# Two graph layers on one core: the message pass as one pipeline, the verdict beside the last strip, and normalising on ScalarE

## The chip, the cores and the metric

One core of a Trainium2 chip runs the whole program. The metric is the device time of one execution in microseconds (us). Differences of about 0.2% (5 us) are the least that a measurement of this kernel can tell from no change.

## The reference

6250 nodes with 128 features, 200,000 edges sorted by target node `dst` (skewed: low nodes have many edges), 32 attributes for each edge.

```python
edge_index = stack([src, dst])
h = maximum(layernorm(x), 0)
x = x + L0(h, edge_index)            # gcn_conv, relu, gcn_conv
h = maximum(layernorm(x), 0)
x = x + L1(h, edge_index, edge_attr)
# gcn_conv: segment_sum((x @ W)[src] * dinv[src] * dinv[dst], dst) + b, self loops included
# L1:  msg = relu(concat(x[src], edge_attr) @ W1 + b1)
#      agg = segment_sum(msg, dst) / max(count, 1)
#      relu(concat(x, agg) @ W2 + b2)
```

## The kernel before, in words

The program is one chain of stages, written out engine by engine. SP, ACT and POOL issue DMAs; order on each engine is the order of the code, and engines meet only at semaphores.

1. **Setup** (to about 240 us): node starts are searched in the sorted target list, features of the first layernorm are made, and a slot is worked out for each of the first 98,304 edges (24 ranges of 32 tiles of 128 edges).
2. **Counts and first convolution** (240 to 960 us): `shared(0)` builds, strip by strip (25 strips of up to 256 targets), a matrix of edge counts (L1083 on PE, one-hots on DVE at L2067 and L2071, eviction on ACT at L1416), and applies it to the node table (L1095). The last strip is short (112 targets) and is applied alone, 49 blocks of 3 matmuls.
3. **Verdict** (`verdict`, L2151 to L2170): DVE checks that the counts are exact, that every range fits, and so on; two small matmuls on PE (L1161, L1162) gather what the partitions found; the result is `flag`. Every engine waits for `flag_ready` 4 and reads the flag: 0 (the case here) takes the fast path, 1 a general one (`full`).
4. **Second convolution**: `node_phase(1)` and `shared(1)`, which loads the stored counts, widens them (L578, L580) and multiplies (L1110), to 1290 us.
5. **Third node phase** (`node_phase(2)`, 1290 to 1362 us, 13 groups of 4 node blocks): for each group PE turns the sums back (`back`), DVE adds x (L1906), takes mean and variance (L1714, L1719), ACT takes the root (L1336), DVE inverts it (L1880) and normalises with four instructions (L1885); PE turns (L947), ACT applies relu twice (L1346, L1349), PE multiplies (L983), DVE adds the bias and makes the rows of the message table (L1919), SP stores them, ACT clears (L1372).
6. **Messages** (`messages_mixed`, 1360 to 2447 us). Two kinds of work run interleaved.
   - *Ranges.* The 98,304 edges whose rows POOL has **scattered** into blocks (L814: 24 ranges x 32 indirect DMAs, issued between stages 2 and 5 with `pace` waits that keep them from running ahead). A range is 49 tiles, handled in 14 **units** of 4 or 3 tiles, 24 x 14 = 336 units. Per unit: ACT stages the attributes (L1511), PE turns them (L1211), ACT takes them (L1518), PE makes products and picks source rows by a one-hot (L1218, L1222; the one-hot on DVE at L2249), ACT and DVE split the message (L1525, L2239), DVE builds the target one-hot (L2254), PE sums (L1234). Per range: the blocks are loaded by SP (`load_blocks`, L634), prepared on DVE (L1892), their low parts turned on PE, stored and loaded again spread over the partitions by ACT (`store_lows`, `load_lows`, L1500), and the sums folded, turned and added.
   - *Chunks.* The other 102,400 edges, 200 chunks of 4 tiles. POOL **gathers** each tile's source rows with one indirect DMA (`gather_messages`, L796: 800 of them), at most 8 chunks ahead of their use and held further by `rows_added` and `pre_ready`. Per chunk: half of an 8-matmul group on PE (L1187), DVE adds (L2262), ACT relu (L1505), one-hot (L2211), PE sums (L1196), DVE adds into the result (L2219).
   - *Order.* `pair_of` writes the order of two ranges (28 units) as 30 **steps**, with 16 chunks spread over them. A hardware loop (`Fori`) runs it 11 times, and a twelfth copy has the last pair with 24 chunks. Steps 28 and 29 of each pair only finish what steps 26 and 27 began, and the next pair's first unit starts behind them. The spread low parts of the next pair's first range are loaded at steps 27, 28 and 29; those of the second range at steps 10, 12 and 14. POOL's 800 gathers are written out, without a loop.
7. **Last phase** (2450 to 2495 us): the update matmuls (L1289, L1292) and the output.

Of the kernel before, what the change touches and what calls it, by code (L numbers as in the profile page):

```python
# [6 lines left out]
F32 = mybir.dt.float32  # L7
# [8 lines left out]
P = 128  # L16
# [74 lines left out]
LO_TURNED_AT = (7, DU + 10)  # L91
LO_LOADED_AT = ({DU - 4: (0, 1), DU - 2: (2,), DU: (3,)}, {2 * DU - 1: (0, 1), 2 * DU: (2,), 2 * DU + 1: (3,)})
FIRST_TURN = DT // (SLOTS * TC)
PAIRS = RANGES // 2
PAIR_UNITS = 2 * DU
PAIR_TURNS = 2
PAIR_CHUNKS = PAIR_TURNS * SLOTS
LAST_CHUNKS = (TURNS - FIRST_TURN) * SLOTS - (PAIRS - 1) * PAIR_CHUNKS
MESSAGE_CHUNKS = (PAIRS - 1) * PAIR_CHUNKS + LAST_CHUNKS
PAIR_STEPS = PAIR_UNITS + 2  # L100
PREPARED_AT = (5, DU + 8)
# [32 lines left out]
EXACT = 256.0  # L134
EPS = 1e-5
# [3 lines left out]
assert DT % (SLOTS * TC) == 0 and LAST_CHUNKS % SLOTS == 0 and RANGES % 2 == 0 and DU % 2 == 0 and sum(UNIT_TILES) == SB and RT % 2 == 0  # L139
# [7 lines left out]
def build(nc, t, out):  # L147
    with ExitStack() as ctx:
# [203 lines left out]
        rstd = sb("rstd", [P, 2, GB])  # L352
        eps = sb("eps", [P, 1])
# [170 lines left out]
        def chunk_of(u, chunks):  # L524

            c = u * chunks // PAIR_STEPS
            return c if (u + 1) * chunks // PAIR_STEPS > c else None
# [55 lines left out]
        def _(sp):  # L583
# [49 lines left out]
            def load_blocks(k, j):  # L633
                sp.dma_start(landed[j], permuted[bass.ds(k * (2 * RANGE_ROWS) + j * RANGE_ROWS, RANGE_ROWS), :].rearrange("(p b) c -> p b c", p=P)  # L634
                             ).then_inc(B[f"landed_{j}"], 16)
# [5 lines left out]
            def load_mixed():  # L641

                def load_pair(k, turns, last):
                    for i in range(turns):
                        for h in range(2):
                            sp.wait_ge(rows_added, k * PAIR_CHUNKS + (i * SLOTS + HALF * h + HALF + 2))
                            load_attributes(k * PAIR_TURNS + (i + 1), h)
                            if (i, h) == (1, 0) and not last:
                                sp.wait_ge(B["prepared"], k * 2 + 1)
                                sp.sem_inc(held["sp"], 1)  # L650
                                sp.wait_ge(B["staged"], k * PAIR_UNITS + DU)
                                load_blocks(k + 1, 0)
                    if not last:
                        sp.wait_ge(B["prepared"], k * 2 + 2)
                        sp.sem_inc(held["sp"], 1)
                        sp.wait_ge(B["staged"], k * PAIR_UNITS + PAIR_UNITS)
                        load_blocks(k + 1, 1)

                for j in range(2):
                    sp.wait_ge(scattered[j], RANGES // 2 * RT * 16)  # L660
                with sp.Fori(0, PAIRS - 1) as k:
                    load_pair(k, PAIR_TURNS, False)
                load_pair(PAIRS - 1, LAST_CHUNKS // SLOTS - 1, True)
# [76 lines left out]
            load_blocks(0, 0)  # L740
            sp.dma_start(message_rows, t["src_t"][:, DT:NT]).then_inc(message_inputs_loaded, 16)
            load_blocks(0, 1)
# [152 lines left out]
        def _(pe):  # L895
# [218 lines left out]
            def shared(n):  # L1114
# [4 lines left out]
                if n == 0:  # L1119
# [20 lines left out]
                    for h in range(SB):  # L1140
                        apply((STRIPS - 1) % 2, h, LAST_WIDTH)
# [18 lines left out]
            pe.wait_ge(flag_ready, 1)  # L1160
            mm(ps_turn[0:1, 0:P], found[:, 0:1], ident, start=True, stop=True).then_inc(flag_ready, 1)  # L1161
            mm(ps_extra[0:1, 0:1], found[:, 3:4], ones[:, 0:1], start=True, stop=True).then_inc(flag_ready, 1)  # L1162
            pe.wait_ge(flag_ready, 4)
            flagged = pe.value_load(flag[0:1, 0:1], min_val=0, max_val=1)
            with pe.If(flagged > 0):
                full(0)
            node_phase(1)
# [4 lines left out]
            def messages_mixed():  # L1172
# [6 lines left out]
                def products_of(k, c):  # L1179

                    pe.wait_ge(rows_added, k * PAIR_CHUNKS + c + 2)
                    if c % HALF == 0:
                        pe.wait_ge(attr_loaded[c % SLOTS // HALF], (k * PAIR_TURNS + c // SLOTS) * 16 + 16)
# [7 lines left out]
                def sums_of(k, c):  # L1191
                    pe.wait_ge(msgs_ready, k * PAIR_CHUNKS + c + 1)
                    pe.wait_ge(e["added"], k * PAIR_CHUNKS + c + SLOTS)
                    pe.wait_ge(e["onehot"], k * PAIR_CHUNKS + c + 1)
# [5 lines left out]
                def turn_lows(k, r):  # L1200

                    pe.wait_ge(B["prepared"], k * 2 + r + 1)
                    pe.wait_ge(B["added"], k * 2 + r + 1)
                    pe.wait_ge(B["lo_evicted"], k * 2 + r + 1)
                    mm(ps_turn[0:SB, 0:P], block_lo[r][:, 0:SB], ident_bf[:], start=True, stop=True).then_inc(B["lo_turned"], 1)

                def turn_attr(k, u):

                    n = unit_tiles(u % DU)[1]
                    pe.wait_ge(B["staged"], k * PAIR_UNITS + u + 1)  # L1210
# [3 lines left out]
                def block_products(k, u):  # L1214

                    b0, n = unit_tiles(u % DU)
                    pe.wait_ge(B["attr"], k * PAIR_UNITS + u + 1)
                    mm(banks[u % 3][:, 0:n * D], attr_turned[u % 2][0:n * DE, :], edge_w[0:n * DE, 0:n].rearrange("p j d -> p (j d)"),  # L1218
                       start=True, stop=False, skip_group_check=True)
                    pe.wait_ge(B["source"], k * PAIR_UNITS + u + 2)  # L1220
# [5 lines left out]
                def block_sums(k, u):  # L1226

                    n = unit_tiles(u % DU)[1]
                    pe.wait_ge(B["rest"], k * PAIR_UNITS + u + 1)
                    pe.wait_ge(B["target"], k * PAIR_UNITS + u + 1)  # L1230
                    if u % DU == 0:
                        pe.wait_ge(B["folded"], k * 2 + u // DU + 1)
# [5 lines left out]
                def turn_sums(k, before, before_lows=True):  # L1238

                    pe.wait_ge(B["folded"], k * 2 + before + 1)  # L1240
                    pe.wait_ge(B["added"], k * 2 + before + 1)
                    if before_lows:
                        pe.wait_ge(B["lo_evicted"], k * 2 + before + 2)
                    nc.tensor.transpose(ps_turn[:, 0:P], range_sums, ident).then_inc(B["sums_turned"], 1)

                def pair_of(k, chunks, last):
                    for u in range(PAIR_STEPS):
                        c = chunk_of(u, chunks)
                        if c is not None and c % 2 == 0 and (not last or c + 2 < chunks):
                            products_of(k, c + 2)  # L1250
                        if u < PAIR_UNITS:
                            turn_attr(k, u)
                        if c is not None:
                            sums_of(k, c)
                        if 1 <= u <= PAIR_UNITS:
                            block_products(k, u - 1)
                        if u == TURNED_SUMS_AT:
                            turn_sums(k, 0)
                        if u == DU + TURNED_SUMS_AT:
                            turn_sums(k, 1)  # L1260
                        if 2 <= u:
                            block_sums(k, u - 2)
# [1122 lines left out]
```

## Time and profile before

| | |
|---|---|
| three runs | 2489.32, 2491.26, 2493.92 us; median 2491.26 |
| profiled execution | 2496.99 us, its span 2494.8 us |
| PE busy | 2175.6 us (87%), 15568 matmuls |
| DVE busy | 1886.4 us (76%) |
| POOL busy | 1824.0 us (73%), 1687 instructions |
| ACT busy | 1219.0 us (49%) |

"Busy" counts execution only. An engine's time between two instructions is listed apart, with what ended it (the releaser). "Issue" as a releaser means that the engine waited for nothing that the profile shows: its own instruction stream had to come forward. So an engine that is busy 73% of the time need not have been free for the other 27%.

### The profile page before, as it was taken

Reading aid. Unit: us, or ns where it says so; the run is one execution under the profiler, and the core shown is the slowest. Engines: PE = TensorE matmul, PEld = TensorE weight load, DVE = VectorE, ACT = ScalarE, POOL = GpSimd, SP = SyncE. Lnnn points to the kernel's source line nnn. Section 1 sums busy time; section 2 is a strip of 40 time slices with the busy share of each in tenths; the row PEclk is TensorE's granted clock in tenths of the full one; section 3 lists DMA queues with packets and bytes.
Section 4 is the critical chain, followed back from the end, with each engine's and each line's share of the span. In section 5 each row is a group of like instructions: output and inputs, shape, how many; then the busy total and the mean of one; then the engine's idle time right before and its main releaser. Section 6 shows DMA issues by size and latency. Waiting matters only on the chain.

```text
span 2494.8 us, 47576 instructions
## 1 busy us (share of the span) xinstructions
PE 2175.6 (87%) x15568; PEld 1787.8 (72%) x15569; DVE 1886.4 (76%) x3609; ACT 1219.0 (49%) x3297; POOL 1824.0 (73%) x1687
## 2 busy tenths in 40 slices
PE   0355799999999996899985899999999999999996
PEld 0133689997668995788874677877877877787785
DVE  6999999998889884544447677776777777777776
ACT  5845246665667773555543343433433443444440
POOL 0858777888888877777777777777777776777770
PEclk9666999999999998999997899999999999999998
DMA  9414133343333432688873334334343433434332
GB/s 365 162 41 160 48 125 125 133 156 118 135 136 125 183 128 61 231 306 323 308 263 87 105 117 136 108 117 124 101 127 115 127 109 102 136 101 128 115 91 61
DMA packets 127167, 357.85 MB, mean 143 GB/s; under 512 B 34082, under 2 KB 77831, under 8 KB 117687
## 3 DMA queue, kind: packets, MB, share of 16 engines
q10 hardware_dynamic: 24752, 186.56, 19.8%
q0 software_dynamic: 56880, 85.25, 13.1%
q1 hardware_dynamic: 45369, 84.00, 9.8%
q8 instruction: 83, 1.36, 0.2%
q14 instruction: 83, 0.68, 0.1%
HBM read 229.75 MB, written 125.93 MB: 143 GB/s over the span
## 4 chain that ended last, share of the span: by engine, by line
PE 67%; DVE 15%; DMA 5%; issue 4%; POOL 4%; ACT 4%; DVEq 1%; ACTq 0%; POOLq 0%; SPq 0%
PE ps_feat L1095 6%; PE ps_sum L1196 6%; PE ps_node L1095 6%; PE ps_node L1110 5%; PE ps_feat L1110 5%; DVE region_c L2071 5%; PE ps_extra L1234 5%; PE ps_node L1218 4%; PE ps_node L1222 4%; DMA rows_or_lows<-block_lows 3%; ACT rows L1310 3%; PE ps_sum L1222 3%; PE ps_feat L1218 3%; PE ps_sum L1218 3%; PE ps_feat L1222 3%
## 5 line engine op out<-in xcount | busy, mean ns | idle before, releaser
L814 POOL DMA_INDIRECT permuted<-rows_or_lows,slot_of_edge x768 | 902.3, 1175 | 234.1 <-issue 150.3
L796 POOL DMA_INDIRECT rows<-table,region_a x800 | 788.1, 985 | 278.9 <-issue 223.6
L2071 DVE TENSOR_TENSOR region_c<-iota_key,region_c 128x1568 bf16<-128x1568 f16 (+1 forms) x327 | 355.5, 1087 | 0.0
L1416 ACT ACTIVATE region_a<-pre_banks 128x392 bf16<-128x392 f32 x392 | 194.9, 499 | 144.9 <-PE pre_banks L1083 136.7
L1095 PE MATMUL ps_node<-region_a,region_b 128*128 128x256 bf16 (+1 forms) x1911 | 261.9, 267 | 0.0
L1095 PE MATMUL ps_feat<-region_a,region_b 128*128 128x256 bf16 x1764 | 251.6, 272 | 0.0
L580 DVE CAST wide_counts<-region_a 128x1024 fp32r<-128x1024 bf16 (+2 forms) x163 | 118.8, 732 | 153.3 <-PE ps_feat L1110 61.5
L1234 PE MATMUL ps_extra<-msg_parts,target_hot 128*128 128x256 f32 x1176 | 222.5, 305 | 3.7 <-DVE msg_parts L2239 3.7
L578 ACT ACTIVATE wide_counts<-region_a 128x1024 fp32r<-128x1024 bf16 x150 | 158.6, 1060 | 119.2 <-PE ps_feat L1110 55.1
L1196 PE MATMUL ps_sum<-onehot,rows 128*128 128x64 f32 x1600 | 209.8, 276 | 0.2 <-issue 0.2
L1196 PEld LDWEIGHTS ps_sum<-onehot,rows 128*128 128x128 f32 x1600 | 205.0, 200 | 5.3 <-issue 4.2
L2254 DVE TENSOR_TENSOR target_hot<-consts,region_a 128x512 fp32r<-128x512 f32 x336 | 207.3, 617 | 1.0
L1095 PEld LDWEIGHTS ps_node<-region_a,region_b 128*128 128x128 bf16 x1911 | 175.3, 97 | 27.4
L1095 PEld LDWEIGHTS ps_feat<-region_a,region_b 128*128 128x128 bf16 x1764 | 168.2, 97 | 27.8
L1525 ACT ACTIVATE msg_parts<-ps_node 128x512 fp32r<-128x512 f32 x120 | 65.3, 544 | 214.9 <-PE ps_node L1222 214.9
L1505 ACT ACTIVATE rows<-rows 128x512 f32<-128x512 f32 x200 | 125.0, 625 | 85.1 <-DMA rows_or_lows<-block_lows 52.8
L1234 PEld LDWEIGHTS ps_extra<-msg_parts,target_hot 128*128 128x128 f32 x1176 | 161.7, 191 | 4.5 <-DVE msg_parts L2239 4.1
L2262 DVE TENSOR_TENSOR rows<-rows,pre_banks 128x512 f32<-128x512 f32 x200 | 136.1, 680 | 29.4 <-DMA rows<-table,region_a 29.0
L1110 PE MATMUL ps_node<-wide_counts,table_halves 128*128 128x512 f32 (+1 forms) x686 | 147.0, 375 | 2.1 <-DVE wide_counts L580 2.1
L2249 DVE TENSOR_SCALAR iota_units<-rows_or_lows,consts 128x512 f32<-128x512 bf16 x168 | 83.3, 496 | 86.6 <-PE ps_node L1222 55.9
L1110 PEld LDWEIGHTS ps_node<-wide_counts,table_halves 128*128 128x128 f32 x686 | 122.1, 188 | 26.1 <-issue 1.8
L1525 ACT ACTIVATE msg_parts<-ps_sum 128x512 fp32r<-128x512 f32 (+1 forms) x108 | 59.4, 550 | 164.9 <-PE ps_sum L1222 164.9
(314 smaller groups left out, 4780.9 us busy)
## 6 DMA issues: line engine op xcount, KB each, us to landing
counts<-region_a ACTq DMA_DIRECT2D x23, 3136.0 KB
region_a<-counts ACTq DMA_DIRECT2D x11, 3200.0 KB
region_a<-counts ACTq DMA_DIRECT2D x11, 3072.0 KB
rows_or_lows<-block_lows ACTq DMA_DIRECT2D x72, 448.0 KB
permuted<-region_b SPq DMA_DIRECT2D x25, 833.0 KB, 24.1
region_a<-permuted SPq DMA_DIRECT2D x24, 833.0 KB
rows_or_lows<-edge_cols_in POOLq DMA_DIRECT2D x24, 544.0 KB
region_a<-attr_t_in SPq DMA_DIRECT2D x50, 256.0 KB, 2.9
```

What stands on the lines that cost most here:

```text
L578: nc.scalar.activation(to, of, ACT.Copy).then_inc(widened["act"], 1)
L796: nc.gpsimd.indirect_dma_start(rows[:, s, j * D:(j + 1) * D], None, tables[2], bass.IndirectOffsetOnAxis(ap=message_rows[:, c * TC + j:c * ...
L814: nc.gpsimd.indirect_dma_start(permuted, bass.IndirectOffsetOnAxis(ap=slot_of_edge[:, r * RT + k:r * RT + k + 1], axis=0), edge_rows_of[:, ...
L1095: ins = mm(strip_bank(buf)[:, 0:width], parts[:, h, k], counts[buf][:, h, 0:width], start=(h == 0 and k == 0), stop=(h == SB - 1 and k == ...
L1110: ins = mm((ps_feat if k % 2 else ps_node)[:, 0:width], halves[:, h, j], blocks[:, h - a], start=(h == 0 and j == 0), stop=(h == SB - 1 an ...
L1196: last = mm(ps_sum[0][:, 0:CW], rows[:, c % SLOTS, j * D:(j + 1) * D], onehot[:, c % 2, j, 0:CW], start=(j == 0), stop=(j == TC - 1))
L1218: mm(banks[u % 3][:, 0:n * D], attr_turned[u % 2][0:n * DE, :], edge_w[0:n * DE, 0:n].rearrange("p j d -> p (j d)"), start=True, stop=Fals ...
L1222: last = mm(banks[u % 3][:, j * D:(j + 1) * D], source_hot[u % 2][:, j * P:(j + 1) * P], messages_of[:, b0 + j], start=False, stop=(j == n ...
L1234: last = mm(ps_extra[:, 0:2 * D], target_hot[:, u % 2, j], msg_parts[:, u % 2, j].rearrange("p h d -> p (h d)"), start=(u % DU == 0 and j ...
L1416: nc.scalar.activation(counts[strip % 2][:, :, j * W:j * W + W], count_banks[w % BANKS][:, 0:KEYS].rearrange("p (d h) -> p h d", h=SB), AC ...
L2071: v.tensor_tensor(hot_key(u)[:, :, 0:n], iota_key[:, None, 0:n].to_broadcast([P, UNIT // SIDE, n, SIDE]), keys[:, :, None, :].to_broadcast ...
L2254: v.tensor_tensor(target_hot[:, u % 2, 0:n], iota[:, None, :].to_broadcast([P, n, P]), block_dst[u // DU][:, b0:b0 + n].unsqueeze(2).to_br ...
```

## The change

It has three parts.

**Messages.** The pairs and the loop go. All 336 units are one pipeline of 338 steps, written out, with the 200 chunks spread evenly over them (one for each 1.69 steps; before one for each 1.88, and one for each 1.25 in the last pair). Every range now has the schedule that the second range of a pair had: fold at its step 2, low parts turned at step 7, loaded at steps 10, 12 and 14 of the range before. The prepare of a range is at step 5 of the range before (in old terms step 5 for the second range, 22 for the first). SP issues the blocks' load and the attributes' loads in the order in which their steps come. `gather_messages` isn't changed.

```diff
-LO_LOADED_AT = ({DU - 4: (0, 1), DU - 2: (2,), DU: (3,)}, {2 * DU - 1: (0, 1), 2 * DU: (2,), 2 * DU + 1: (3,)})
+LO_LOADED_AT = {DU - 4: (0, 1), DU - 2: (2,), DU: (3,)}
+MESSAGE_UNITS = RANGES * DU
+MESSAGE_STEPS = MESSAGE_UNITS + 2
+        def chunk_at(step):
+            c = step * MESSAGE_CHUNKS // MESSAGE_STEPS
+            return c if (step + 1) * MESSAGE_CHUNKS // MESSAGE_STEPS > c else None
 # tensor engine
-                with pe.Fori(0, PAIRS - 1) as k:
-                    pair_of(k, PAIR_CHUNKS, False)
-                pair_of(PAIRS - 1, LAST_CHUNKS, True)
-                turn_sums(PAIRS, 0, False)
+                for step in range(MESSAGE_STEPS):
+                    c = chunk_at(step)
+                    r, at = range_step(step)
+                    if c is not None and c % 2 == 0 and c + 2 < MESSAGE_CHUNKS:
+                        products_of(c + 2)
+                    if step < MESSAGE_UNITS:
+                        turn_attr(step)
+                    if c is not None:
+                        sums_of(c)
+                    if 1 <= step <= MESSAGE_UNITS:
+                        block_products(step - 1)
+                    if r < RANGES and at == TURNED_SUMS_AT:
+                        turn_sums(r)
+                    if 2 <= step:
+                        block_sums(step - 2)
+                    if r < RANGES - 1 and at == LO_TURNED_AT:
+                        turn_lows(r + 1)
+                turn_sums(RANGES, False)
 # sync engine
+                for r in range(2, RANGES):
+                    while q is not None and STEP_OF_CHUNK[HALF * q + 1] < (r - 1) * DU:
+                        next_attributes(q)
+                        q = next(quarters, None)
+                    next_blocks(r)
```

**Verdict.** What can be judged without the last strip (`found_ahead`) is done by DVE while PE applies the strip before; after the last counts are evicted `set_flag` adds the rest. PE puts the two small matmuls behind block 16 of the last strip and reads the flag after block 32; the other 17 blocks and DVE's add of the last strip (`last_added`) stand in both branches behind the flag.

```diff
-                    for h in range(SB):
+                    for h in range(FLAG_AT):
+                        if h == FOUND_AT:
+                            pe.wait_ge(flag_ready, 1)
+                            mm(ps_turn[0:1, 0:P], found[:, 0:1], ident, start=True, stop=True).then_inc(flag_ready, 1)
+                            mm(ps_extra[0:1, 0:1], found[:, 3:4], ones[:, 0:1], start=True, stop=True).then_inc(flag_ready, 1)
                         apply((STRIPS - 1) % 2, h, LAST_WIDTH)
...
+            with pe.Else():
+                last_applied()
```

**Third node phase.** DVE makes only the scales, the inverse root and minus mean times it (`scales_of`, one small instruction more); ACT normalises with four `Identity` activations for each group, between `features(g)` and `clear(g)`; DVE makes a group's rows one turn later.

```diff
-                for b in range(GB):
-                    last = v.tensor_scalar(normed[g % 2][:, b], a[:, g * GN + b * P:g * GN + (b + 1) * P],
-                                           moments[:, g % 2, b, 0:1], rstd[:, g % 2, b:b + 1], ALU.subtract, ALU.mult)
-                last.then_inc(G["normed"], 1)
+                v.scalar_tensor_tensor(out=minus_mean[:, g % 2], in0=moments[:, g % 2, :, 0], scalar=-1.0, in1=rstd[:, g % 2],
+                                       op0=ALU.mult, op1=ALU.mult).then_inc(rstd_ready, 1)
 # scalar engine
+                def normalise(g):
+                    act.wait_ge(rstd_ready, NG + 2 * g + 2)
+                    if g >= 2:
+                        act.wait_ge(G["turned"], g + NG - 1)
+                    for b in range(GB):
+                        last = nc.scalar.activation(normed[g % 2][:, b], region_b[:, g * GN + b * P:g * GN + (b + 1) * P], ACT.Identity,
+                                                    bias=minus_mean[:, g % 2, b:b + 1], scale=rstd[:, g % 2, b:b + 1])
+                    last.then_inc(G["normed"], 1)
```

## Rows read from the trace of the kernel before

**Rows 1.** The page: PE and POOL in 40 slices, and the chain's shares.
```profile
PE   0355799999999996899985899999999999999996
POOL 0858777888888877777777777777777776777770
PE 67%; DVE 15%; DMA 5%; issue 4%; POOL 4%; ACT 4%; DVEq 1%; ACTq 0%; POOLq 0%; SPq 0%
```
**Rows 2.** Waits of POOL from 220 to 1369 us: us in total, times, longest us.
```profile
POOL permuted L814 <- issue: 150.3, 493, 0.3
POOL permuted L814 <- ACT region_a L1416: 62.8, 206, 0.3
```
**Rows 3.** Timeline of POOL at its handover from scatters to gathers, and its last gather.
```profile
1368.78 0.96 POOL L814 DMA_INDIRECT permuted<-rows_or_lows,slot_of_edge  x1 [0.31 <-issue]
1370.04 0.98 POOL L796 DMA_INDIRECT rows<-table,region_a  x1 [0.30 <-issue]
...
2435.54 1.14 POOL L796 DMA_INDIRECT rows<-table,region_a  x1 [0.30 <-issue]
```
**Rows 4.** POOL's groups from 1370 to 1760 us, then from 600 to 760 us.
```profile
L796 POOL DMA_INDIRECT rows<-table,region_a x301 | 299.1, 994 | 91.7 <-issue 82.3 <-DVE agg L2219 6.1 <-PE pre_banks L1187 1.8
...
L814 POOL DMA_INDIRECT permuted<-rows_or_lows,slot_of_edge x86 | 135.1, 1571 | 26.2 <-issue 13.7 <-ACT region_a L1416 12.5
```
**Rows 5.** POOL in stretches: us, POOL busy (count), PE clock, DMA share, GB/s.
```profile
1760.00:2345.00 585.00, 419.54 (x429) 0.98 0.40 118
2345.00:2437.00 92.00, 69.99 (x72) 1.00 0.35 90
```
**Rows 6.** Waits of POOL from 1760 to 2345 us.
```profile
POOL rows L796 <- issue: 121.4, 381, 2.1
POOL rows L796 <- PE pre_banks L1187: 35.8, 27, 1.8
```
**Rows 7.** PE's timeline, one pair: steps 3 and 27; step 1 of the next; a chunk's groups.
```profile
1655.74 0.27 PE L1211 MATMUL ps_node<-consts,region_a 128*96 128x128 f32 x1
1724.75 0.27 PE L1211 MATMUL ps_node<-consts,region_a 128*96 128x128 f32 x1
1736.09 0.45 PE L1211 MATMUL ps_feat<-consts,region_a 128*96 128x128 f32 x1 [1.95 <-ACT region_a L1511]
...
1715.52 1.14 PE L1187 MATMUL pre_banks<-edge_w,region_a 64*128 64x256 f32 x8
1716.75 1.00 PE L1196 MATMUL ps_sum<-onehot,rows 128*128 128x64 f32 x8
```
**Rows 8.** PE waits, 1286 to 1384 us.
```profile
PE pre_banks L1187 <- DVE rows L2262: 20.2, 1, 20.2
```
**Rows 9.** Groups from 1290 to 1362 us.
```profile
L1885 DVE TENSOR_SCALAR rows<-region_b,moments,rstd 128x128 f32<-128x128 f32 x52 | 14.8, 361 | 0.5
L1346 ACT ACTIVATE rows<-ps_turn 128x512 f32<-128x512 f32 x7 | 4.2, 597 | 16.8 <-PE ps_turn L947 16.8
L1511 ACT ACTIVATE region_a<-region_a 128x128 f32<-128x128 f32 x1 | 0.3, 310 | 0.0
```
**Rows 10.** Timeline around the verdict, and the store of the last table rows.
```profile
957.62 0.18 DVE L2151 TENSOR_SCALAR range_over<-range_over 128x24 f32<-128x24 f32 x1 [0.16 <-issue]
...
967.71 0.63 ACT L1346 ACTIVATE rows<-agg 128x512 f32<-128x512 f32 x1 [18.72 <-DVEq L2186]
...
1359.35 0.36 SPq L630 DMA_DIRECT2D table<-region_c  x1
```
**Rows 11.** Timeline: a load of blocks on SP and the prepare that waits for it.
```profile
1703.02 0.33 SPq L634 DMA_DIRECT2D region_a<-permuted  x1
1713.03 0.37 DVE L1892 TENSOR_SCALAR region_a<-region_a 128x49 int32<-128x49 int32 x1
```
**Rows 12.** Timeline at the end of the messages.
```profile
2440.73 0.69 DVE L2262 TENSOR_TENSOR rows<-rows,pre_banks 128x512 f32<-128x512 f32 x1 [4.13 <-DMA rows<-table,region_a]
2450.58 2.07 PE L1289 MATMUL ps_node<-upd_w,region_a 128*128 128x128 f32 x8 [3.85 <-DVEq L2316]
```

More of the change, by code:

```diff
@@ L641, in load_mixed, with next_blocks, next_attributes @@
             def load_mixed():
[L643 to L657, printed above, removed]
+                def next_blocks(r):
+                    sp.wait_ge(B["prepared"], r - 1)
+                    sp.sem_inc(held["sp"], 1)
+                    sp.wait_ge(B["staged"], (r - 1) * DU)
+                    load_blocks(r)
+                def next_attributes(q):
+                    sp.wait_ge(rows_added, HALF * q + HALF + 2)
+                    load_attributes(q // 2 + 1, q % 2)
                 for j in range(2):
                     sp.wait_ge(scattered[j], RANGES // 2 * RT * 16)
-                with sp.Fori(0, PAIRS - 1) as k:
-                    load_pair(k, PAIR_TURNS, False)
-                load_pair(PAIRS - 1, LAST_CHUNKS // SLOTS - 1, True)
+                quarters = iter(range(MESSAGE_CHUNKS // HALF - 2))
+                q = next(quarters)
+                for r in range(2, RANGES):
[3 more added lines that the diff above has]
+                    next_blocks(r)
+                while q is not None:
+                    next_attributes(q)
+                    q = next(quarters, None)
             def load_edges(e, messages=False):
@@ L1158, in _, with last_applied @@
             shared(0)
-            pe.wait_ge(flag_ready, 1)
-            mm(ps_turn[0:1, 0:P], found[:, 0:1], ident, start=True, stop=True).then_inc(flag_ready, 1)
-            mm(ps_extra[0:1, 0:1], found[:, 3:4], ones[:, 0:1], start=True, stop=True).then_inc(flag_ready, 1)
+            def last_applied():
+                for h in range(FLAG_AT, SB):
+                    apply((STRIPS - 1) % 2, h, LAST_WIDTH)
             pe.wait_ge(flag_ready, 4)
@@ L1244, in turn_sums @@
                     nc.tensor.transpose(ps_turn[:, 0:P], range_sums, ident).then_inc(B["sums_turned"], 1)
[L1246 to L1262, printed above, removed]
-                        if u == LO_TURNED_AT[0]:
-                            turn_lows(k, 1)
-                        if u == LO_TURNED_AT[1] and not last:
-                            turn_lows(k + 1, 0)
@@ new lines, in messages_mixed @@
+                message(0)
+                for step in range(MESSAGE_STEPS):
+                    c = chunk_at(step)
+                    r, at = range_step(step)
+                    if c is not None and c + 1 < MESSAGE_CHUNKS:
+                        message(c + 1)
+                    if step + 1 < MESSAGE_UNITS:
+                        stage_attr(step + 1)
+                    if step < MESSAGE_UNITS:
+                        take_attr(step)
+                    if 1 <= step <= MESSAGE_UNITS:
+                        block_message(step - 1)
+                    if r < RANGES - 1 and at == LO_TURNED_AT + 1:
+                        store_lows(r + 1)
+                    for of, since in ((r + 1, at), (r, at + DU)):
+                        if 0 < of < RANGES:
+                            for i in LO_LOADED_AT.get(since, ()):
+                                load_lows(of, i, (of - 1) * DU + (min(LO_UNITS * (i + 1), DU) + 1))
@@ L1966, in node_phase @@
                     mean_and_variance(region_b, n, 0)
-                    normalise(region_b, n, 0)
-                    for g in range(NG + 1):
+                    scales_of(0)
+                    for g in range(NG + 2):
                         if g + 1 < NG:
@@ L2182, in _ @@
             shared(0)
-            flagged = verdict()
+            flagged = dve.value_load(flag[0:1, 0:1], min_val=0, max_val=1)
             with dve.If(flagged > 0):
+                last_added()
                 full(0)
+            with dve.Else():
+                last_added()
             dve.sem_inc(G["sums"], 1)
```

346 lines of the change are left out of this document (161 added, 185 removed).

## The prediction, made blind

> **What bounds the kernel now.** I read the page first. PE is at 9 in nearly every slice and has 67% of the chain; POOL has 7 or 8 and 4% of the chain [rows 1]. That invites the view that PE bounds everything and that whatever PE idles for is won. I then asked what POOL waits for, since its 1568 indirect DMAs are long, few and one behind the other. From 220 to 1369 us no wait of POOL is longer than 0.3 us, neither where its own stream comes forward nor behind the pace waits [rows 2]. 0.30 us stands between any two of its DMAs, waiting or not [rows 3]; it is the price of issuing. So POOL is full, and its slices show 7 or 8 only because those 0.30 us are not counted as busy. The last scatter starts at 1368.78 and the first gather at 1370.04, one step later; 800 gathers follow, the last from 2435.54 to 2436.68 [rows 3]. In the first 390 us of them POOL has again nothing but 0.30 us gaps: 301 gathers, 299.1 busy + 91.7 idle = 390.8 us, **1.298 us each** [rows 4]. In the last 92 us it is 72 gathers, 1.278 us each [rows 5]. Only between 1760 and 2345 us does it wait for others: 27 waits for the products on PE, 35.8 us, of which 27 x 0.30 = 8 would be there anyhow, and 7 us above 0.30 in the 381 others (121.4 - 381 x 0.30) [rows 6]. In all about 35 to 37 us.
>
> So POOL runs from 220 to 2437 us and stands still for some 36 us of it. PE waits for POOL at the start of the messages (20.2 us, for the first rows [rows 8]), leads by being held back (POOL reaches its limit of eight chunks after 1760), and DVE waits for the last gather to land (4.13 us, behind which come the last sums and the last phase at 2450.58 [rows 12]). From the end of the last gather to the end of the span it is 2494.8 - 2436.68 = 58.1 us.
>
> **Messages, on PE.** In the interior of a pair PE never stops: 24 steps in 1724.75 - 1655.74 = 69.01 us, 2.875 us each [rows 7], with 24 x 16/30 = 12.8 chunks in them. A chunk costs PE the L1196 group and half an L1187 group, 1.00 + 0.57 = 1.57 us [rows 7]; a unit then costs (69.0 - 12.8 x 1.57)/24 = 2.04 us. The seam between two pairs is what the change removes: from step 27 of one to step 1 of the next it takes 1736.09 - 1724.75 = 11.3 us for four steps of which two are half empty, with PE idle for 1.95 us [rows 7] and slower behind it. The new pipeline needs 338 x 2.04 + 200 x 1.57 = 1003 us on PE. Its second step starts at 1384 as now (set by the first rows), so PE alone would be through at 2387 instead of about 2446. **That is the gain that PE promises: 59 us.**
>
> **Messages, on POOL.** `gather_messages` is the same, and 800 gathers at 1.298 us are 1038 us. They start behind the last scatter, 1370.0, and end at **2408.4** rather than 2436.7: 28.3 us. POOL needs 4 x 1.298 = 5.19 us for a chunk, PE 1.69 x 2.04 + 1.57 = 5.02. POOL is the slower by 3%, so it is never held by its limits, and PE, ACT and DVE fall in step with it. I take 1.298 and not 1.278 (ends 2392) because the first comes from the longer stretch with nearly the new chunk rate; the bounds are 1.278 and, from the other stages, 1.87 ((135.1 + 26.2)/86, counts on DVE [rows 4]), to which I come below.
>
> **The tail.** Behind the last gather DVE adds at the step of chunk 197, which is step 334; a full unit (step 335) and the rests of 336 and 337 follow. Before, chunk 21 of 24 lay at step 27 and only steps 28 and 29 followed. One unit more, 2.0 us at most as PE can do part of it while it waits; bounds 0 and 3. I take 2.0.
>
> **Preparing a range.** SP loads a range's blocks about when the range two before is staged, and DVE prepares at step 5: six steps, over 15 us. The trace has such a load issued at 1703.02 with its prepare run at 1713.03, in ten us and without a stall [rows 11]. The low parts come at steps 10, 12 and 14, as the second range of a pair has them now without a stall of PE. Nothing is added; were a load later than its prepare, DVE stops, and behind it the one-hots of the next units, 22 times. Attributes are asked for some eight steps ahead of their use, and stay hidden.
>
> **Code without loop.** POOL's is straight already. For the others the loop's counters and computed addresses go, which saves part of the seam's time; bounds 0 and the seam itself, which is in PE's sum.
> The Trainium skill (Runtime: NRT & Kernel Launch, Instruction fetch mechanics) says that fetching is sequential and that a taken branch out of the window stalls the engine. By that the loop's seams hold a fetch as well. The seam above shows PE idle behind ACT, not behind its own fetch, and the sum is the same by either, as POOL sets it.
>
> **Verdict.** From 957.6 to 967.7 us PE and ACT stand still for the flag [rows 10]; the change takes up to 9 of these 10.1 us off that path (bounds 0 and 9). All of it lies beside POOL's scatters: at 1290 us, when the second convolution ends, POOL still has 79 us of them. POOL reads the flag itself only behind its seventeenth range, when seven ranges, 224 scatters at 1.26 us or more [rows 3], are still to come: between 1020 and 1088 us, long after the flag is there. Worth 0, and nothing that comes earlier can take POOL's place.
>
> **Third node phase.** DVE loses 52 instructions, 14.8 us [rows 9], and gets 13 tiny ones (2 us); ACT gets 52 of about 0.30 us (the nearest row is 128x128 at 0.310 [rows 9]), 15.6 us, on a chain ACT, PE, ACT in each group. Bounds for the phase: 13 us shorter and, if that chain sets the pace, 7 longer. The last table rows are stored from 1359.35 on [rows 10], the scatters end at 1369.7: 7 us of cover for the store to land, and up to 9 more from the verdict. Worth 0. Without the cover it would be those 7 us.
>
> **Sum.** 2408.4 + 58.1 + 2.0 = 2468.5 us of span. Around the span the profiled execution has 2496.99 - 2494.8 = 2.2 us: 2470.7. That execution lies 5.7 us above the median; taking that off, **2465 us**, 26 us or 1.1% faster.
>
> **Rivals.**
> *A. PE is right (12%).* If POOL is held less in the new rhythm and comes near 1.25 us a gather (rows at the handover are 1.26 apart [rows 3]), it would end at 2370 and PE's 2387 sets the end. 59 us less and 2 more of tail: 2434 at the best, some 2440 with POOL still a little in the way. For it: the 72 gathers at 1.278 [rows 5]. Against: the rows at the handover stand beside an idle DVE, and 1.278 is the best of the long stretches.
> *B. Slower: DVE takes POOL's time (8%).* A gather lasts 0.94 to 1.4 us on POOL, a scatter 1.571 on average beside the one-hots of the counts [rows 4]. So something on DVE slows POOL, and the change packs the same DVE work for the messages into less time, with no quiet seams. Its place is L796; it decides from (2436.7 - 2.0 - 1370.0)/800 = 1.333 us a gather, at which all is lost. A rise to 1.37 gives 1096 us, an end at 2466, 29 us later than now, and with 2 of tail 2522. Against: in the stretch of 301 DVE was as dense already but for the seams, and its slow gathers are counted.
> The Trainium skill (SBUF — State Buffer, SBUF: two separate sides) has the mechanism: DVE and GpSimd share a port pair that one of them holds for a whole instruction, and POOL cannot write its descriptors meanwhile. By that the time lost goes with the number of DVE instructions of the kind, which the change leaves alone here, and the sum stands; the rows show only that DMAs differ in length from stage to stage.
> *C. No change, within 5 us (7%).* The in-order engines catch on each other: units come with one or two to a chunk (3.6 or 5.7 us of PE for 5.19 of POOL), and the loads of blocks have less room than now. If PE falls behind by the 3% that it has in hand, POOL waits as it does now: 2486 to 2494.
> *The verdict and the node phase count (3%).* If POOL had slack, they would give up to 20 us on top. Rows 2 speak against.
>
> **How the numbers follow.** The forecast has 70%. Its own range is 1.285 to 1.315 us a gather, 2455 to 2479. The range of 8 in 10 takes in part of A and the near side of C: **2445 to 2484**. Faster by over 0.2% (5 us, about the least that can be told from nothing here): forecast, A and the last rival, 0.85; within, 0.07; slower, 0.08.
>
> **What would show it.** POOL: no wait above 0.3 us from 1380 us to the end of the gathers, 1.29 to 1.31 us each, the last near 2408. PE: no seam; small waits for L2262 or L1505 chunk by chunk, busy near 96%. PE's wait for the first rows longer than 20.2 us, by what the verdict and the node phase saved, with the first gather still at 1370. I am wrong if the first gather moves by over 2 us, if POOL waits again for PE, or if a gather costs under 1.28 or over 1.32.

## The result, and the profile after

The kernel after needs **2464.2 us** (median of 4 runs, 2462.0 to 2468.9) where the kernel before, beside it, needs 2492.45: a ratio of 0.9891, 95% interval 0.9873 to 0.9909. Its profiled execution took 2462.0 us, with a span of 2460.1. On a second chip the same kernel had 0.9875 (0.9857 to 0.9893).

The page after, the rows that answer to [rows 1]: PE and POOL in 40 slices, and the chain's shares.
```profile
PE   0344899999999998799995599999999999999996
POOL 0867877888888787777777777777777777777770
PE 52%; POOL 17%; DVE 15%; issue 8%; ACT 4%; DMA 3%; DVEq 1%; POOLq 0%; ACTq 0%; SPq 0%
```
The digits look the same. What moved is the chain: POOL has 17% of it instead of 4%.

POOL's waits after, from 220 to 2460 us: us in total, times, longest us [rows 2, 6].
```profile
POOL rows L803 <- issue: 236.8, 777, 0.3
POOL permuted L821 <- issue: 151.7, 498, 0.3
POOL permuted L821 <- ACT region_a L1435: 63.1, 207, 0.3
...
POOL rows L803 <- PE pre_banks L1203: 3.7, 12, 0.3
POOL rows L803 <- DVE agg L2244: 1.8, 6, 0.3
```
No wait is longer than 0.3 us in 2200 us. The 35.8 us behind L1187 of [rows 6] have become 3.7 in 12 times 0.3, which is the price of issuing.

POOL's timeline after, at the handover and at the last gather [rows 3], and its group over the messages [rows 4, 5].
```profile
1369.83 0.95 POOL L821 DMA_INDIRECT permuted<-rows_or_lows,slot_of_edge  x1 [0.30 <-issue]
1371.09 0.99 POOL L803 DMA_INDIRECT rows<-table,region_a  x1 [0.30 <-issue]
...
2399.74 0.94 POOL L803 DMA_INDIRECT rows<-table,region_a  x1 [0.30 <-issue]
```
```profile
L803 POOL DMA_INDIRECT rows<-table,region_a x800 | 786.1, 983 | 243.8 <-issue 236.8 <-PE pre_banks L1203 3.7 <-DVE agg L2244 1.8
```
800 gathers take 786.1 + 243.8 = 1029.9 us, **1.287 us each**, from 1371.1 to 2400.7. Before they took 788.1 + 278.9 = 1067.0. A gather's own time is the same in both kernels (983 ns here, 985 before; half of all gathers take under 0.95 us in either, and 116 and 114 of the 800 take over 1.05 us, up to 1.46); only the standing still between them has gone.

PE's waits after, from 1286 to 1384 us [rows 8, 9], and then from 1395 to 2400 us [rows 7].
```profile
PE pre_banks L1203 <- DVE rows L2287: 30.2, 1, 30.2
PE ps_turn L954 <- ACT rows L1352: 10.2, 6, 6.1
```
```profile
PE ps_extra L1250 <- DVE msg_parts L2264: 12.1, 13, 2.6
PE pre_banks L1203 <- DVE rows L2287: 1.1, 1, 1.1
PE ps_turn L1260 <- DVE onehot_x L2250: 1.1, 1, 1.1
```
The wait for the first rows has grown by 10 us: the node phase ends earlier and PE only waits longer for POOL. In the messages the seam's wait for ACT is gone. PE is busy for 787.57 of 800 us (778.10 in the same stretch of the kernel before):
```profile
1500.00:2300.00 800.00, 787.57 (x5440) 1.00 0.42 124
```
ACT's group with the new normalising, the last table store, ACT's first step behind the verdict, and the last phase (PE), all after [rows 9, 10, 12].
```profile
L1352 ACT ACTIVATE rows<-region_b,minus_mean,rstd 128x128 f32<-128x128 f32 x52 | 21.3, 486 | 0.8 <-DVE minus_mean L1894 0.8
...
1351.47 0.36 SPq L634 DMA_DIRECT2D table<-region_c  x1
...
963.80 1.15 ACT L1364 ACTIVATE rows<-agg 128x512 f32<-128x512 f32 x2 [14.55 <-DVEq L2212]
...
2415.87 2.08 PE L1297 MATMUL ps_node<-upd_w,region_a 128*128 128x128 f32 x8 [3.81 <-DVEq L2334]
```
The last rows of the table are stored 7.9 us earlier (1351.47 for 1359.35), and the step behind the verdict begins 3.9 us earlier (963.80 for 967.71). Neither moves the first gather. Of the verdict's 3.9 us little reached even PE, whose second convolution starts 0.4 us earlier (the first rows of L1117 after and of L1110 before):
```profile
1010.84 3.47 PE L1117 MATMUL ps_node<-wide_counts,table_halves 128*128 128x512 f32 x8 [1.59 <-DVE wide_counts L584]
```
```profile
1011.28 2.99 PE L1110 MATMUL ps_node<-wide_counts,table_halves 128*128 128x512 f32 x12 [1.59 <-DVE wide_counts L580]
```

### The profile page after: what moved, and what is told of

Same layout as the page of the kernel before. It is cut to its first block, busy times and chain, and to the rows that moved or that the text cites. A ratio compares the mean times of both kernels' runs of the same rounds, so it can differ in the third digit from the quotient of the medians.

```text
span 2460.1 us, 45677 instructions
## 1 busy us (share of the span) xinstructions
PE 2155.0 (88%) x15568; PEld 1771.9 (72%) x15569; DVE 1870.1 (76%) x3574; ACT 1241.6 (50%) x3349; POOL 1822.6 (74%) x1687
## 4 chain that ended last, share of the span: by engine, by line
PE 52%; POOL 17%; DVE 15%; issue 8%; ACT 4%; DMA 3%; DVEq 1%; POOLq 0%; ACTq 0%; SPq 0%
POOL rows L803 14%; PE ps_feat L1102 6%; PE ps_node L1102 6%; PE ps_node L1117 5%; PE ps_feat L1117 5%; DVE region_c L2079 5%; PE ps_sum L1212 3%; ACT rows L1318 3%; PE pre_banks L1090 3%; PE ps_extra L1250 3%; POOL permuted L821 2%; PE pre_banks L1203 2%; PE ps_feat L1234 2%; PE ps_node L1234 2%; PE ps_sum L1234 2%
## 5 line engine op out<-in xcount | busy, mean ns | idle before, releaser
L803 POOL DMA_INDIRECT rows<-table,region_a x800 | 786.1, 983 | 243.8 <-issue 236.8
L1212 PE MATMUL ps_sum<-onehot,rows 128*128 128x64 f32 x1600 | 202.3, 270 | 0.0
L1117 PE MATMUL ps_node<-wide_counts,table_halves 128*128 128x512 f32 (+1 forms) x686 | 148.6, 377 | 2.0 <-DVE wide_counts L584 1.9
L1544 ACT ACTIVATE msg_parts<-ps_feat 128x384 fp32r<-128x384 f32 x112 | 61.0, 545 | 175.7 <-PE ps_feat L1238 175.7
L1544 ACT ACTIVATE msg_parts<-ps_sum 128x512 fp32r<-128x512 f32 x112 | 61.0, 545 | 170.4 <-PE ps_sum L1238 170.4
L1203 PE MATMUL pre_banks<-edge_w,region_a 64*128 64x256 f32 x800 | 114.4, 405 | 32.3 <-DVE rows L2287 31.3
```

Of the source, the lines that this page charges most:

```text
L803: nc.gpsimd.indirect_dma_start(rows[:, s, j * D:(j + 1) * D], None, tables[2], bass.IndirectOffsetOnAxis(ap=message_rows[:, c * TC + j:c * ...
L1117: ins = mm((ps_feat if k % 2 else ps_node)[:, 0:width], halves[:, h, j], blocks[:, h - a], start=(h == 0 and j == 0), stop=(h == SB - 1 an ...
L1203: last = mm(pre_halves[:, half, q], attr[part, (c + q) % SLOTS], edge_w[part, half * 2:half * 2 + 2].rearrange("p j d -> p (j d)"), start= ...
L1544: nc.scalar.activation(msg_parts[:, u % 2, 0:n, 0], banks[u % 3][:, 0:n * D].rearrange("p (j d) -> p j d", d=D), ACT.Relu).then_inc(B["msg ...
```

## The experiments

Theory 1 is that of the prediction: GpSimd's (POOL's) own stream sets the end, and the messages' pipeline wins what POOL stood still for. e1 to e4 shared one chip with the kernel before, whose median there was 2489.2 us; e5 to e8 a second (2490.1), and e9 to e12 a third (2493.7). The kernel after ran beside e1 to e4 only (as e3), so the others are set against it by their ratios to the kernel before. The code below is shown in part.

**1 to 3: which part wins.** Messages alone, verdict and node phase alone, and the whole change again.
```
 e1: the change without its verdict and node-phase parts
-    FOUND_AT, FLAG_AT = 16, 32; last_applied(); ACT's normalise(g); DVE's scales_of(g)
 e2: the kernel before, with exactly these parts
+    FOUND_AT, FLAG_AT = 16, 32; last_applied(); ACT's normalise(g); DVE's scales_of(g)
     with dve.Fori(0, PAIRS - 1) as k:      # the messages stay in the loop over pairs
```


> The messages as one pipeline, with the verdict and the third node phase as before. Theory 1 (POOL's scatters and gathers, one behind the other, set the end; the verdict and the node phase lie beside them): the whole gain, 2465 us, first gather at 1370, 800 gathers at 1.287 us. Rival (PE's path sets the end): the 4 us of the verdict and the 9 us of the node phase are missing, 2477 us.

Measured: 2459.5 us, ratio 0.9876 (0.9852 to 0.9901).

> The changed kernel again, beside the others on one chip: 2464 us.

Measured: 2459.2 us, 0.9875 (0.9857 to 0.9893). The messages are the whole gain; the other two parts add 0.3 us, which is nothing.

> The verdict beside the last strip and the normalising on ScalarE, with the messages in pairs as before. Theory 1: no change, 2492 us (2489 to 2495), PE's wait for the first rows longer by about 10 us than the 20.2 of before, first gather still at 1370. Rival (PE's path sets the end): 13 us faster, 2479 us.

Measured: **2525.2 us, 1.0151 (1.0127 to 1.0174)**, 36 us slower than before. No theory had this. What POOL stands still above its 0.30 us between gathers has grown from 35 to 57 us. (The two profiled executions are only 24 us apart in their spans, 2518.6 for 2494.8: that of e2 lay 5 us below its median, that of the kernel before 6 above the median that was forecast from.) The waits of DVE in this kernel, from 1470 to 2340 us, and its timeline where a new turn of the loop begins:
```profile
DVE agg L2257 <- issue: 36.3, 20, 2.3
...
DVE onehot L2249 <- issue: 26.1, 20, 3.2
DVE iota_units L2287 <- issue: 22.7, 10, 2.9
```
```profile
1473.59 0.70 DVE L2287 TENSOR_SCALAR iota_units<-rows_or_lows,consts 128x512 f32<-128x512 bf16 x1 [2.26 <-issue]
1474.21 0.40 DVE L2287 TENSOR_SCALAR slot_of_edge<-rows_or_lows,consts 128x384 f32<-128x384 bf16 x1
1476.45 0.42 DVE L2249 TENSOR_TENSOR onehot<-consts,dst_rel 128x256 f32<-128x256 f32 x1 [1.84 <-issue]
1476.79 0.68 DVE L2292 TENSOR_TENSOR target_hot<-consts,region_a 128x512 fp32r<-128x512 f32 x1
1479.76 0.22 DVE L2257 TENSOR_TENSOR agg<-agg,ps_sum 128x64 f32 x1 [2.29 <-issue]
```
Three stalls of about 2 us on nothing but its own issue, in every turn, in code that the edit did not touch. The expectation of e5 speaks of 24 turns; the loop has 11. I took the stalls for fetches of code; the view of the DMA queues counts those. Queue 14 (instruction packets) from 1480 to 2340 us, packets, MB, share: first this kernel, then the kernel before.
```profile
q14 instruction: 54, 0.44, 0.2%
```
```profile
q14 instruction: 8, 0.07, 0.0%
```

**4: POOL started earlier.** GpSimd waits for others in the setup (11.4 and 5.6 us, two rows below, of the kernel after from 130 to 240 us); twelve scatters of the first range are put there.
```
+            pool.wait_ge(blanked, 16 * (RANGES + 1)); pool.wait_ge(ranked, 1); pool.wait_ge(rows_staged[0], 16)
+            scatter_tiles(0, range(8))
             pool.wait_ge(starts_moved, 16)
...
+            scatter_tiles(0, range(8, 12))
             pool.wait_ge(visit_rows_ready, 1)
...
-                for k in range(RT):
+                for k in range(12 if r == 0 else 0, RT):
```
```profile
POOL visit_start L855 <- DMA starts_of_nodes<-starts_i: 11.4, 1, 11.4
...
POOL region_a L861 <- DVE visit_row L1883: 5.6, 1, 5.6
```


> The changed kernel with 12 of the first range's 32 scatters issued by POOL while it waits in the setup (8 in its wait of 11.4 us for the starts, 4 in its wait of 5.6 us for the rows). Nothing else is touched. Theory 1: POOL is 12 x 1.3 = 15.6 us ahead from then on, the first gather comes at 1355.5 us and the end 15.6 us earlier, 2449 us, unless the last table rows (stored from 1351.5 on, 2.3 us to land) hold the first gather. Rival (PE's path sets the end): no change, 2464 us; PE's wait for the first rows does not shrink.

Measured: **2446.3 us, 0.9827 (0.9809 to 0.9845)**, 12.9 us less than the kernel after on that chip. It beats both kernels. The first gather and the last, here:
```profile
1357.05 0.98 POOL L803 DMA_INDIRECT rows<-table,region_a  x1 [0.31 <-issue]
...
2382.90 0.94 POOL L803 DMA_INDIRECT rows<-table,region_a  x1 [0.30 <-issue]
```
Against e3, the kernel after on the same chip (first gather at 1370.21, last at 2399.23, span 2459.3 us), the handover is 13.2 us earlier, the last gather 16.3, the span 15.9. Work taken off POOL at 140 us comes out at the end, 2300 us later, nearly whole.

**5 and 6: no-operations ahead of the loop.** They were meant to move DVE's loop code.
```
             with dve.If(flagged > 0):
                 full(1)
+                for _ in range(32):          # e5, on the kernel of e2; 230 in e6, on the kernel before
+                    dve.nop()
```


> The same edit as the run of verdict and node phase alone (2525.2 us, 36 us slower than before), with 32 no-operations of VectorE put into a branch that is not taken, ahead of the messages' loop: nothing more is executed, the loop's code only lies 32 instructions further on. Theory A (VectorE fetches the loop's code anew in each of the 24 turns because of where its code lies): the stalls of 2 to 3 us at the start of each turn go or shrink, about 2489 (2480 to 2496). Theory B (the moved verdict or ScalarE's normalising costs the 36 us itself): 2525 again (2518 to 2532).

Measured: 2523.9 us, 1.0123 (1.0098 to 1.0149), five runs of which one took 2542.9.

> The kernel before, with 230 no-operations of VectorE in a branch that is not taken, ahead of the messages' loop. Theory A: if the position of the loop's code is what costs, some positions must cost the kernel before as much as the run of verdict and node phase alone lost: 2525 (2510 to 2535), with VectorE idle on its own issue at the start of each turn. Theory B: 2489 (2484 to 2494), as nothing executed has changed. A third outcome, 2489 with the padded run above repaired, would say that the position matters but that this one is a good one.

Measured: 2492.3 us, 1.0011 (0.9994 to 1.0028). Neither says anything on the position: the compiler drops these no-operations, and the compiled loops begin at the same instructions as without them (3172 and 3202). Both runs are repeats, and as such they show that the loss is no accident of a chip: 34 us on this one.

**9 and 10: the code really moved.** The same place, with real instructions that are never executed.
```
             with dve.If(flagged > 0):
                 full(1)
+                for _ in range(60):          # e9, on the kernel of e2; 90 in e10, on the kernel before
+                    v.memset(mixed_f[:], 0.0)
```


> Verdict and node phase alone (2525 us), with 60 real instructions of VectorE (tiny memsets) in the branch that is not taken. In the compiled code VectorE's loop of 307 instructions (64 bytes each) began at instruction 3202 before, at 3172 in the run of verdict and node phase alone, and begins at 3232 here; VectorE's instruction packets are of 8 KB, 128 instructions, so that the loop lies over three such blocks before (offset 2), over four in the slow run (offset 100), and over three here (offset 32). Theory A (four blocks are fetched anew in each turn, three are kept): the stalls go, 2489 (2483 to 2495). Theory B (the moved verdict or ScalarE's normalising costs the 36 us): 2525 (2518 to 2532).

Measured: **2493.1 us, 0.9996 (0.9978 to 1.0014)**. The whole loss is gone. DVE's waits of 1470 to 2340 us, and queue 14 of 1480 to 2340 us:
```profile
DVE agg L2259 <- PE ps_sum L1207: 66.0, 70, 3.1
...
DVE agg L2259 <- issue: 13.7, 10, 1.4
```
```profile
q14 instruction: 9, 0.07, 0.0%
```


> The kernel before with 90 real instructions of VectorE in the branch that is not taken: its loop begins at instruction 3292, offset 92 in a block of 128, and lies over four blocks. Theory A: VectorE stalls on its own issue at the start of each turn and the kernel needs 2525 us (2510 to 2535) though nothing more is executed. Theory B: 2489 (2484 to 2494).

Measured: **2508.4 us, 1.0064 (1.0043 to 1.0084)**: slower with not one instruction more executed, though by 15 us and not by 36, and so just under the range that theory A gave. The same two views:
```profile
DVE agg L2221 <- issue: 47.0, 20, 4.0
...
DVE iota_units L2251 <- issue: 21.5, 9, 3.3
```
```profile
q14 instruction: 54, 0.44, 0.2%
```
So where the code lies decides whether a turn fetches it anew, and the moved verdict and node phase cost nothing: e9 is their real worth, 0. e10 moves VectorE's code alone, and queue 14's count goes with it, so the added packets are VectorE's. Over the whole execution queue 14 has 83 packets in the kernel before and in e9, and 132 in e2 and e10: 49 more in 11 turns, 4.5 a turn. Packets by themselves don't seem to cost: the kernel after, written out without a loop, has 46 of them on queue 14 in the same stretch, and DVE idles there on issue for 29 us in all, where it is 23 in the kernel before and 91 in e2. What e2 and e10 have besides is the jump back to code that has to be fetched first.

The count of packets is the same at both bad positions and the loss is not; in the lines shown DVE idles on issue for 69 us here and for 85 in e2 (14 of them in the kernel before as well), and which steps those stalls fall on differs too. How a position makes 15 us or 36 wasn't settled.

**7 and 8: POOL relieved.** Every chunk's fourth gather is left out.
```
-                    for j in range(TC):
+                    for j in range(TC - 1):
-  dve.wait_ge(e["gathered"][c % SLOTS], ... * (16 * TC))
+  dve.wait_ge(e["gathered"][c % SLOTS], ... * (16 * (TC - 1)))
```


> The kernel after without the fourth gather of each chunk, so 600 gathers in place of 800 (a quarter of the source rows is stale; TensorE's, VectorE's and ScalarE's work is whole). Theory 1 (GpSimd's 1.29 us per gather sets the messages' length, 1030 us): GpSimd then needs 772 us, TensorE's own 1003 us become the bound, and the time falls by about 20 us, to 2440 (2434 to 2448). Rival A (TensorE is already the bound after the change): within 3 us of the kernel after, 2459.

Measured: **2439.2 us, 0.9790 (0.9767 to 0.9814)**. POOL now waits (from 1380 to 2340 us 150.6 us for DVE's adds alone), and PE, busy for 799.20 of the 800 us from 1500 on, is the bound:
```profile
POOL rows L803 <- DVE rows L2287: 150.6, 130, 2.7
POOL rows L803 <- issue: 125.4, 360, 4.7
POOL rows L803 <- PE pre_banks L1203: 99.6, 72, 2.4
```
```profile
1500.00:2300.00 800.00, 799.20 (x5564) 1.00 0.38 113
```


> The kernel before without the fourth gather of each chunk. With GpSimd out of the way only the loop's seams are left beside TensorE's 1003 us. Theory 1 (the seams cost nothing much by themselves, they cost by making GpSimd wait some 36 us): the time falls too, to about 2475 (2462 to 2484), and the distance to the same kernel after is the worth of the seams to TensorE, about 35 us. Rival A (the seams hold TensorE and GpSimd is hidden beside them): 2489, unchanged.

Measured: 2473.1 us, 0.9925 (0.9900 to 0.9949). With POOL out of the way the loop's seams are worth 2473.1 - 2439.2 = 34 us to PE. With all gathers they are worth 30, as POOL's stream allows no more. In the kernel before, relieving POOL alone wins 17 us (2490.1 - 2473.1), taking out the seams alone wins 30, both together 51. I read that as PE's seams and POOL's full stream taking turns as the bound.

**11: POOL has less to do ahead of the messages.** The 32 scatters of the last range are left out.
```
-                        for j, r in enumerate(beside):
+                        for j, r in enumerate(beside[:-1]):
```


> The kernel after without the 32 scatters of the last range (the last range's rows are stale; everything else is done), so that GpSimd has 40 us less to do ahead of the messages. Theory 1 (GpSimd's own work sets when the first gather starts, the node phase ends unseen beside it): the first gather moves from 1371 us to the end of the table's store, about 1354, GpSimd then waits for the node phase, and the time falls by 16 us, to 2443 (2438 to 2449). Rival (the gathers' start does not set the end): within 3 us of the kernel after, 2459.

Measured: 2448.9 us, 0.9818 (0.9782 to 0.9854), at the very edge of what was expected, from four runs that lie 10 us apart. POOL's last scatter and first gather there:
```profile
1329.05 0.96 POOL L821 DMA_INDIRECT permuted<-rows_or_lows,slot_of_edge  x1 [0.30 <-issue]
1358.05 0.98 POOL L803 DMA_INDIRECT rows<-table,region_a  x1 [28.05 <-DMA table<-region_c]
```
Now the node phase is the start. Against the profile of the kernel after (another chip) the first gather comes 13.0 us earlier, the last ends 11.5 earlier (2389.2), the span is 11.3 shorter. I had put the gather at 1354: the last store is issued at 1352.89 in this kernel, and 5.2 us lie between that and the gather. The same 5.2 us behind the kernel before's 1359.35 would give 1364.5, still 5.5 us ahead of its handover at 1370.0. The cover was real, and thinner than the 7 us that I had counted on.

**12: does DVE slow POOL?** The target one-hots are left out from the third unit on.
```
+                    if u >= 2:
+                        v.tensor_copy(target_hot[:, u % 2, 0, 0:1], iota[:, 0:1]).then_inc(B["target"], 1)
+                        return
```


> The kernel after with VectorE's target one-hots (336 instructions of 0.62 us, a fifth of VectorE's load beside the messages) left out from the third unit on, replaced by a copy of one column. Rival B (VectorE's accesses slow GpSimd's gathers): a gather's own time falls from 979 ns towards 940, and the time goes to TensorE's bound, about 2440. Theory 1 (GpSimd's 0.98 and 0.30 us are its own in this stage): a gather's own time stays at 979 ns, the time within 5 us of 2459.

Measured: 2443.4 us, 0.9808 (0.9777 to 0.9840). POOL's gathers in that kernel:
```profile
L803 POOL DMA_INDIRECT rows<-table,region_a x800 | 763.7, 955 | 243.9 <-issue 227.1 <-DVE agg L2244 8.5 <-PE pre_banks L1203 4.9
```
A gather is 955 ns for 983, with the same 0.30 us behind it: 786.1 - 763.7 = 22.4 us over 800. The median gather is the same (0.947 us in both); what has gone are long ones, 28 over 1.05 us in place of 116. So rival B's mechanism is there: 334 instructions of 0.62 us on average, 207 us of DVE, cost POOL 22 us, some 0.11 us for each us (their stand-ins, 334 copies of one column, took 48 us of DVE). It is a part of the 1.287 us in both kernels, and so of neither's difference. Theory 1 as I had written it for this run (a gather's 0.98 us are its own) fell. The Trainium skill (SBUF — State Buffer, SBUF: two separate sides) has DVE and GpSimd share a port pair; this run agrees in direction, with 28 ns a gather, and shows no more of how.

## Why the prediction was right

**The bound.** Right. [Rows 2] against the page's digits decided it. e4 and e11 show that POOL's work ahead of the messages sets their start. By themselves they would fit a PE that sets the pace from there on, as PE too starts earlier in them; that POOL sets the pace is shown by e7 and e12, where the start stays or comes later and a shorter stream of POOL shortens the kernel, until PE is busy for 799 of 800 us.

**Messages on POOL.** Mechanism right, size off by 8 us. A gather took 1.287 us, not 1.298. I had taken the mean of the 301 gathers of [rows 4]; the best stretch of [rows 5], which I gave as a bound, was 1.278, and the truth is about in the middle. The rows of before held it: the other line of [rows 5] has 419.54 us for 429 gathers, 978 ns each, and all 800 gathers of the kernel before have 985 ns of their own, 1.290 us with the 0.305 behind each. 800 x 0.0106 = 8.5 us, less 1.05 for a handover at 1371.1 instead of 1370.0: the last gather ended at 2400.7 where I had 2408.4. The first 301 gathers of the kernel before are its slow ones, 994 ns of their own in [rows 4] against 979 for the other 499, and my sum took them for all. (Rival B's line, too, had a slip: (2436.7 - 2.0 - 1370.0)/800 is 1.331 and not 1.333.)

**Messages on PE.** The 59 us promised were nearly right as a floor: e7 has 334 steps in 2381.96 - 1384.93 = 997.0 us (its second and last L1227 rows), 2.985 each, against 1003/338 = 2.967. Rival A's 2434 to 2440 is just what e7 gives at 2439, once POOL is relieved; with all gathers it did not happen. PE was in the kernel after 98% busy and not 96: the two engines are some 2% apart (4 x 1.287 = 5.15 us a chunk for POOL, 1.69 x 2.985 = 5.04 for PE), closer than my 3%. Nor does PE wait chunk by chunk for the adds, as I wrote: its one wait of weight is 12.1 us for L2264, and it is DVE that stands ahead of the gathered rows.

**Tail.** From the end of the last gather to the end of the span 59.4 us, for 58.1 before: 1.3 more, I had 2.0.

**Preparing a range.** No wait of PE for it showed. DVE does wait 46.2 us for gathered rows, the sign that POOL leads.

**Code without loop.** Here I was right for these two kernels and lucky in the position. I bounded it by nothing and the seam, and said that the seam showed PE behind ACT, not behind a fetch. That holds for the kernel before, where VectorE's loop lies well; e2 and e10 show that the same seam can cost 36 or 15 us more, on DVE, which I had not looked at for it. The Trainium skill (Runtime: NRT & Kernel Launch, Instruction fetch mechanics) had warned of a stall at such a branch, and I set the warning aside on one profile; that the place of the code decides it, e9 and e10 had to show.

**Verdict.** Worth 0, right (e1 against e3, and e9). Its step was 3.9 us shorter, within my 0 to 9, and hardly any of that reached the second convolution. Most of the rest went where the prediction had no term: behind the flag that it now reads in the middle of the last strip, PE stood 3.22 us and then 0.85 us on its own issue (from 955.35 and 962.02 us on).

**Third node phase.** Worth 0, right. The store came 7.9 us earlier, within my bounds of 13 shorter to 7 longer; ACT's normalising cost 21.3 us for 52 and not 15.6, as I had taken 0.30 us from L1511, a copy without bias and scale.

**The sum.** A span of 2460.1 for 2468.5: 8.4 less, 7.7 by the gathers and 0.7 by the tail. The median came out at 2464.2 for 2465 because a second error cancelled it: I took off 5.7 us for a profiled execution above the median, and this time it lay 2.2 below. Of the nearness of the two numbers some 8 us is luck. The gain came out at 28 us for 26 by the medians, and at 34.7 by the spans of the two profiled executions (37.1 by POOL's stream, less 1.0 for the handover and 1.3 for the tail), since before's was a long one; that it is a gain of 1.1 to 1.4%, and POOL's, isn't luck.

## What to carry to other kernels

An engine at 7 in every slice can be the bound: ask what it waits for, and count as work the gap that stands between any two of its instructions. A gain on the engine that looks full is capped by the one that is full; work it out as a sum of its own, and buy the next gain there (twelve scatters in a setup wait gave 13 us more). Moving code without changing it can cost a loop 1.5% (e2 against e9); when an edit loses time in lines it did not touch, look for idle "issue" at the start of each turn and for instruction packets, and move the code before judging the edit.

## What the runs showed of the hardware

- VectorE's loop is 307 instructions of 64 bytes, 19.6 KB, in packets of 8 KB (0.44 MB in 54), which are 128 instructions. It was fetched anew in each turn, at 36 and 15 us in all, where it begins 30 instructions before its place in the kernel before (e2) and 90 behind it (e10): 54 packets on queue 14 in 860 us. In that place and 30 behind it (e9) there were 8 and 9. In blocks of 128 that fits three blocks held and four not: wherever between 0 and 29 instructions into a block the loop of the kernel before begins, the two good positions lie over three blocks and the two bad ones over four. The expectations give 2 for it; that count depends on what of the compiled file is counted, the distances don't. Four positions are all that was tried. The Trainium skill (same section as above) speaks of blocks of 16 KiB, two at a time, and of a stall where a branch leads out of them. The stall agrees, the size does not: in blocks of 256 instructions no beginning of the loop puts the two bad positions over more blocks than the two good ones.
- An indirect DMA costs GpSimd 0.30 us of issue between two, in every stage of these kernels, and in the messages 0.94 us of its own at the least, 0.98 on average and up to 1.46. Of the average 0.03 is the price of VectorE's target one-hots, and it comes as a few long gathers, not as a little on each.
